# Softplus of a state-space kernel: its raw values copied to SBUF first, Exp and Ln kept in du, one clip for two row blocks

## The reference

```python
u = silu(conv(x @ W_in))
dbl = u @ W_x                      # 64 columns for dt, 16 for B, 16 for C
delta = softplus(dt @ W_dt + b_dt)
h = exp(delta * A) * h + (delta * u) * B      # over 2048 -> 4 x 512 tokens
y = sum over the 16 states of h * C
y = (y + u * Dp) * silu(res)
out = y @ W_out
```

## Time and profile before

| | |
|---|---|
| median of 3 runs | 2071.01 us (2067.32 to 2074.3) |
| profiled execution: its own time | 2073.18 us |
| its span, first to last instruction | 2071.5 us |
| mean granted TensorE clock | 0.971 of full speed |
| TensorE, matmuls | 1850.7 us busy, 89% |
| VectorE | 1564.5 us, 76% |
| ScalarE | 1464.7 us, 71% |
| GpSimd | 1538.3 us, 74% |

### The profile page before, as it was taken

How to read it: one execution, slowest core, us unless ns; L and a number is a source line. 1 busy time by engine, 2 the same in 40 slices (tenths; PEclk the granted TensorE clock), 3 DMA queues, 4 the chain that set the end, 5 groups by cost and what they waited for, 6 DMA issues and landing times.

```text
span 2071.5 us, 31985 instructions
## 1 busy us (share of the span) xinstructions
PE 1850.7 (89%) x12240; PEld 1465.2 (71%) x12240; DVE 1564.5 (76%) x1703; ACT 1464.7 (71%) x2467; POOL 1538.3 (74%) x896
## 2 busy tenths in 40 slices
PE   6989899999999999999999999999898986779994
PEld 3447677777777777777777777777677775669893
DVE  1358989798989897979798988888888887752232
ACT  0268888888888888888878787878797884613231
POOL 0039898889898988888888888888989896750331
PEclk9989999999999999999999999999999998899997
DMA  7211111111111111110111111111111112152542
GB/s 248 101 51 43 52 43 61 43 62 43 62 43 62 43 61 43 48 55 34 62 41 63 41 63 42 63 41 63 42 63 41 53 52 72 62 178 85 226 144 91
DMA packets 46394, 144.27 MB, mean 70 GB/s; under 512 B 7009, under 2 KB 18529, under 8 KB 42914
## 3 DMA queue, kind: packets, MB, share of 16 engines
q1 hardware_dynamic: 41538, 114.97, 16.2%
q0 software_dynamic: 4704, 27.27, 3.7%
HBM read 119.67 MB, written 22.54 MB: 69 GB/s over the span
## 4 chain that ended last, share of the span: by engine, by line
PE 52%; DVE 19%; issue 12%; ACT 12%; POOL 2%; DMA 2%; SPq 0%; DVEq 0%; POOLq 0%; ACTq 0%
PE b_ps L1316 12%; DVE hid L1043 10%; PE y_all L1327 9%; ACT dub_t L694 6%; ACT hid L681 5%; DVE u L851 4%; PE bank_b L1199 3%; PE bank_a L1449 3%; PE y_all L1118 3%; PE bank_b L1214 3%; PE bank_a L1223 3%; PE b_ps L1434 2%; PE y_all L1434 2%; PE bank_a L1247 2%; PE bank_a L1214 2%
## 5 line engine op out<-in xcount | busy, mean ns | idle before, releaser
L1043 DVE TENSOR_TENSOR_SCAN hid<-hid,b_ps 128x512 f32<-128x512 f32 x1024 | 1218.3, 1210 | 243.2 <-PE b_ps L1316 222.8
L504 POOL TENSOR_TENSOR hid<-hid,c_rep 128x1024 f32<-128x1024 f32 x512 | 1210.3, 2383 | 221.5 <-DVE hid L1043 221.5
L1316 PEld LDWEIGHTS b_ps<-ident,dub_t 128*128 128x128 f32 x4096 | 488.7, 143 | 375.5 <-issue 231.1
L1316 PE MATMUL b_ps<-ident,dub_t 128*128 128x128 f32 x4096 | 634.9, 278 | 78.9 <-DVE hid L1043 74.9
L681 ACT ACTIVATE hid<-delta,neg_a 128x512 f32<-128x512 f32 x1024 | 652.7, 710 | 0.2
L1327 PE MATMUL y_all<-ident,hid 128*128 128x128 f32 x4096 | 620.6, 275 | 3.8 <-POOL hid L504 3.8
L694 ACT ACTIVATE dub_t<-du_t,b_t 128x512 f32<-128x512 f32 x768 | 490.2, 711 | 54.8 <-PE b_ps L1316 53.1
L1327 PEld LDWEIGHTS y_all<-ident,hid 128*128 128x128 f32 x4096 | 485.7, 143 | 4.8 <-POOL hid L504 4.8
L495 POOL TENSOR_SCALAR dub_t<-du_t,b_t 128x512 f32<-128x512 f32 x256 | 173.8, 707 | 0.0
L1199 PE MATMUL bank_b<-xn,w_in_sb 128*128 128x512 f32 x256 | 134.5, 612 | 15.6 <-DVE xn L838 12.5
L851 DVE SCALAR_TENSOR_TENSOR u<-bank_b,conv_w_sb,u 128x511 f32<-128x511 f32 (+2 forms) x192 | 139.4, 726 | 0.7
(11 more groups left out here) (210 smaller groups left out, 1613.1 us busy)
## 6 DMA issues: line engine op xcount, KB each, us to landing
c_rep<-bc_dram SPq DMA_DIRECT2D x128, 512.0 KB, 3.6
hid<-x_t SPq DMA_DIRECT2D x4, 2048.0 KB, 8.8
xt<-x_dram SPq DMA_DIRECT2D x15, 512.0 KB, 3.6
x_dram<-x_out SPq DMA_DIRECT2D x15, 512.0 KB, 2.9
z_dram<-du SPq DMA_DIRECT2D x2, 1408.0 KB, 18.9
y_dram<-hid SPq DMA_DIRECT2D x22, 128.0 KB, 2.0
h_dram<-hid SPq DMA_DIRECT2D x4, 512.0 KB, 3.9
x_dram<-hid SPq DMA_DIRECT2D x3, 512.0 KB, 2.7
```

The source lines that it names most:

```text
L504: nc.gpsimd.tensor_tensor(part, part, c_rep[:, n % 2, s % GROUP, :].unsqueeze(1) .broadcast_to([P, HALF, SEQ]), ALU.mult).then_inc(hc_read ...
L1043: nc.vector.tensor_tensor_scan(hid[:, i % RING, d, :], hid[:, i % RING, d, :], b_ps[d % 2][:, :], 0.0, ALU.mult, ALU.add)\
L1316: last = nc.tensor.transpose(b_ps[d % 2][:, c * P:(c + 1) * P], dub_t[:, i % DUB, c, d * P:(d + 1) * P], ident[:, :])
```

## The change

ScalarE copies each W_dt product from PSUM to `delta` (its own semaphore `delta_in`), and that copy frees the bank for all that waited for the clip before. For each half (two row blocks) Exp then goes from `delta` to `du`, Ln in place in `du`, each as one instruction of 1024 elements a partition. The clip takes both operands from SBUF (`delta` and `du`), also one instruction for a half. ScalarE does all of this in one place of its list, ahead of the B products of state 9. The slots move: W_dt products 2 and 3 to (7, 0) and (7, 1), clips to (7, 1) and (7, 3), the norm's spread to (8, 1), normalise to (8, 2), `times_u` of the first half behind the first C product of state 7, and of the second half behind the first C product of state 8. The wait for `du` to be free goes from `times_u` to Exp.

```diff
@@ GpSimd
                         pool.wait_ge(delta_ready, NI * k + HALF * (half + 1))
                         if k:
                             pool.wait_ge(dut_done, TC * k)
-                        else:
-                            pool.wait_ge(z_zeroed, 2 * 16)
...
-                                if live(k + 1) and (s, half) == (6, 1):
+                                if live(k + 1) and (s, half) == (7, 0):
                                     times_u(k + 1, 0)
-                                if live(k + 1) and (s, half) == (7, 1):
+                                if live(k + 1) and (s, half) == (8, 0):
                                     times_u(k + 1, 1)
@@ ScalarE
-                    def delta_exp(k, d):
+                    def delta_copy(k, d):
                         act.wait_ge(wdt_done, NI * k + d + 1)
-                        nc.scalar.activation(delta[:, k % 2, d, :], (bank_a if d % 2 == 0 else bank_b)[:, :], ACT.Exp)\
-                            .then_inc(exp_ready, 1)
-
-                    def delta_log(k, d):
-                        act.wait_ge(exp_ready, NI * k + d + 1)
-                        nc.scalar.activation(delta[:, k % 2, d, :], delta[:, k % 2, d, :], ACT.Ln, bias=1.0).then_inc(log_ready, 1)
+                        nc.scalar.activation(delta[:, k % 2, d, :], (bank_a if d % 2 == 0 else bank_b)[:, :], ACT.Copy).then_inc(delta_in, 1)
+
+                    def delta_exp(k, half):
+                        rows = slice(half * HALF, (half + 1) * HALF)
+                        act.wait_ge(delta_in, NI * k + HALF * (half + 1))
+                        if k:
+                            act.wait_ge(dut_done, TC * k)
+                        else:
+                            act.wait_ge(z_zeroed, 2 * 16)
+                        nc.scalar.activation(du[:, rows, :], delta[:, k % 2, rows, :], ACT.Exp).then_inc(exp_ready, 1)
+
+                    def delta_log(k, half):
+                        rows = slice(half * HALF, (half + 1) * HALF)
+                        act.wait_ge(exp_ready, 2 * k + half + 1)
+                        nc.scalar.activation(du[:, rows, :], du[:, rows, :], ACT.Ln, bias=1.0).then_inc(log_ready, 1)
...
                             if s == 8 and live(k + 1):
-                                delta_exp(k + 1, 0)
-                                delta_exp(k + 1, 1)
-                                delta_log(k + 1, 0)
-                                delta_log(k + 1, 1)
+                                for half in range(2):
+                                    delta_copy(k + 1, 2 * half)
+                                    delta_copy(k + 1, 2 * half + 1)
+                                    delta_exp(k + 1, half)
+                                    delta_log(k + 1, half)
...
-                            if s == 8 and live(k + 1):
-                                delta_exp(k + 1, 2)
-                                delta_exp(k + 1, 3)
-                                delta_log(k + 1, 2)
-                                delta_log(k + 1, 3)
@@ VectorE
-                    def softplus(k, d):
-                        dve.wait_ge(log_ready, NI * k + d + 1)
-                        nc.vector.scalar_tensor_tensor(delta[:, k % 2, d, :], (bank_a if d % 2 == 0 else bank_b)[:, :], 60.0,
-                                                       delta[:, k % 2, d, :], ALU.max, ALU.min).then_inc(delta_ready, 1)
+                    def softplus(k, half):
+                        rows = slice(half * HALF, (half + 1) * HALF)
+                        dve.wait_ge(log_ready, 2 * k + half + 1)
+                        nc.vector.scalar_tensor_tensor(delta[:, k % 2, rows, :], delta[:, k % 2, rows, :], 60.0, du[:, rows, :],
+                                                       ALU.max, ALU.min).then_inc(delta_ready, HALF)
...
-                    SOFTPLUS_AT = {(7, 0): 0, (7, 1): 1, (8, 0): 2, (8, 1): 3}
+                    SOFTPLUS_AT = {(7, 1): 0, (7, 3): 1}
...
-                                if live(k + 2) and at == (8, 3):
+                                if live(k + 2) and at == (8, 2):
                                     normalize(k + 2)
@@ TensorE (delta_in for delta_ready also in du_turn, back and h_turn)
                         if k:
-                            pe.wait_ge(delta_ready, NI * k)
+                            pe.wait_ge(delta_in, NI * k)
...
                         if d >= 2:
-                            pe.wait_ge(delta_ready, NI * k + d - 1)
+                            pe.wait_ge(delta_in, NI * k + d - 1)
...
-                    WDT_AT = {(6, 1): 0, (6, 2): 1, (7, 1): 2, (7, 2): 3}
+                    WDT_AT = {(6, 1): 0, (6, 2): 1, (7, 0): 2, (7, 1): 3}
...
-                                if live(k + 2) and at == (8, 2):
+                                if live(k + 2) and at == (8, 1):
                                     spread_norm(k + 2)
```

More of the change, by code:

```diff
@@ L205, in build @@
             wdt_done = sem("wdt_done")
+            delta_in = sem("delta_in")
             exp_ready = sem("exp_ready")
@@ L1252, in du_turn @@
                             pe.wait_ge(du_ready, 2 * (k + 1))
-                            pe.wait_ge(delta_ready, NI * k + 3)
+                            pe.wait_ge(delta_in, NI * k + 3)
                             if k >= 2:
@@ L1265, in back @@
                         if dc == 0 and not live(k + 2):
-                            pe.wait_ge(delta_ready, NI * STEPS)
+                            pe.wait_ge(delta_in, NI * STEPS)
                             if k:
@@ L1273, in back @@
                         if dc == 2 and live(k + 2):
-                            pe.wait_ge(delta_ready, NI * (k + 2) + 3)
+                            pe.wait_ge(delta_in, NI * (k + 2) + 3)
                         if dc == 2 and not live(k + 2) and k:
```

## The result

The changed kernel took 2082.93 us (median of 4 runs, 2077.37 to 2085.82); the kernel before took 2069.16 us beside it (4 runs, 2064.63 to 2074.30). The ratio is 1.0065, 95% interval 1.0045 to 1.0084: slower by 0.65%. The number lies inside the range given (2048 to 2083), at its very end, but outside the likeliest case's own range (2062 to 2078), and the case forecast, no change that can be measured, did not happen.

The account below looks back on a forecast made before the run. No engine was full; each slot lasted as long as the slower of TensorE's and VectorE's lists. 9 x (1.64 - 1.6) + 5 x (1.76 - 1.6) = 1.2 us gained, about 0.8 in all, gave 2070 us, range 2048 to 2083.

Parts of the forecast that it names:

- the likeliest case: Whole kernel: a gain of about 0.8 us, about 2070 us, own range 2062 to 2078, chance 0.55.
- The bound and what is removed: TensorE's stalls for the clip at the third W_dt product, back 2 and the norm's spread go: 3.1 us a step.
- the walk: Part-by-part pass through one step, engine by engine; TensorE reaches the du turn at (9,2) about 2.7 us earlier if unobstructed.
- ScalarE: Four narrow copies and four wide instructions of 1.1 add 2.3 us a step, hidden ahead of the clips.
- GpSimd's chain: GpSimd from state 6's last product to du complete: 14.40 us + x; a step gains 1.64 - x, or 1.76 - x.
- x: Time the two wide clips take from GpSimd a step: 1.4 to 1.8 us, taken as 1.6, bounds 0 and 2.2.
- rival 2: GpSimd from state 7 to du's second half becomes the bound; x 2.2 to 2.4, 2078 to 2081 us; chance 0.18.
- VectorE waits about 2 us, but this is hidden: At the second clip, if GpSimd issues first; TensorE is then at the turn at 724.4, still before du.
- The last step: Last of the sixteen steps, without normalise, GpSimd behind all the way: loses up to 0.4 us.
- The clock: Granted clock dips in five of fourteen steps; the change shifts this, from no dips (-8) to all fourteen (+14 us).
- rival 3: TensorE's idle stretches at (8,2) or (9,2) grow to 3 us, more steps dip: up to 2085 us; chance 0.10.

## Why the prediction was wrong

**The bound and what is removed: right.** The three bank stalls are gone. Once du is in time and no clip is held up, a step is 102.0 to 102.4 long instead of 104.4, and 101.7 with clips of one operand, which is the 2.7 us that the walk gave.

**ScalarE: right.** Each wide Exp and Ln lasts 1.06 (taken 1.1), and no clip of the full steps waits for one.

**GpSimd's chain: right in form.** The prediction had 14.40 us + x, with gains of 1.64 - x and 1.76 - x; at x = 0 the runs gave 1.62 and 1.71. In the steps with the dip x is 0.90 + 1.04 = 1.94, so a loss of 0.18 was due, and 106.23 against 106.07 is 0.16.

**The size of x: this is the step that failed**, and with it the sign. The prediction took 1.6 as the likeliest, since "a short instruction slips in between two of GpSimd's in about 0.4 us that cost nothing", from the earlier trace rows. That row was an instruction of 0.40 us that reads one tensor, and it was carried over to clips of 1.2 that read two. Nor does it show a free place in between: the two of these instructions that met the products at 1796.95 lasted 1.57 and 2.42, and each ended 0.15 us after the product beside it. The clips cost GpSimd 0.9 to 1.04 each wherever they got in, with no discount: in the step of the result section without a dip 1.16 (du waiting for the clip) + 0.99 = 2.15. The chain is 16.3 to 16.6 us long, which the prediction's own mark of 16.2 calls rival 2. The rival had the right place and mechanism, with a chance of 0.18; its x of 2.2 to 2.4 was a little too large. With the measured x the prediction's own formulas give, over the 13 steps, 7 x (2.15 - 1.64) + 6 x (1.94 - 1.76) = 4.7 us lost instead of 1.2 gained. That settles the sign, but it is only about half of the 9.2 measured; the other half is the clock, below.

**"VectorE waits about 2 us, but this is hidden": wrong as well.** The prediction allowed this for the second clip only; it happened to the first, in 8 of 14 steps, and du's first half had to wait for it. Nor is it hidden: TensorE has scans to feed behind it and pauses 3.2 us, and this cost 2.9 us a step even where du was in time. For the second clip, where it alone had two SBUF operands, the same: 4.31 us of pause. The prediction put this wait of TensorE at nothing; it is most of the 23.4 us more ahead of the B transposes.

**The last step: mis-sized.** "Loses up to 0.4" was 3.9. The new order alone accounts for 2.1 of it (102.58 against 100.45), with du behind its turn.

**The clock: in part rival 3.** One more dip after the squares, 1.8 us. Beyond that, what the rival had named: pauses of over 3 us in one piece, behind which the clock falls. Windows of 2 us from two turns at which TensorE had waited 3.17 (us, TensorE's busy us, clock, DMA share, GB/s):

```profile
624.30:626.30 2.00, 2.00 (x18) 1.00 0.00 0
626.30:628.30 2.00, 2.00 (x20) 1.00 0.00 0
307.21:309.21 2.00, 2.00 (x15) 0.79 0.00 0
309.21:311.21 2.00, 2.00 (x11) 0.50 0.00 0
```

Behind the turn at 624.30 the clock stayed, behind that at 307.21 it fell to half. It fell behind four of the six waits of 3.15 to 3.32, and the steps that follow these four are 105.8 long, where the others of their kind are 104.95 to 105.2; that is about 3 us. What decides between the two wasn't found, and it isn't the length of the wait alone: with only the first clip on two operands it fell behind a wait of 2.36 (turn at 1456.84; 0.50 from 1458.84 to 1460.84), and in the changed kernel's repeat it stayed at 1.00 behind waits of 3.40 and 3.44 (turns at 1470.78 and 204.52). Nor is it settled why the version with du's old places has no dip at all; the last 8 of its 32.6 us can't be counted on.

**The Trainium skill**, "SBUF — State Buffer", section "Who interferes with whom", says that an instruction of VectorE with two SBUF inputs contends with one of GpSimd that reads SBUF, that the second to issue is blocked fully, and that a `tensor_reduce` never contends. The runs agree: 1.19 us for each reduce, and 38.6 us between the two clips. In one point they differ: it says that the order of issue decides, and the clip issued at 924.39 let the product that started at 924.64 go first. The prediction cited the rule and then granted a discount from a row of another instruction. The rule speaks of two instructions; what a queue of them does to the one that waits, 3.73 to 8.27 us for 1.2 us of work, is what the experiments add.

## What to carry over

An operand moved from PSUM to SBUF can cost more than the stall it removes: look up what GpSimd reads beside the instruction, charge the full overlap in both directions, and as the worst case charge the waiting engine with every GpSimd instruction queued behind the current one. If such an instruction can't be avoided, put GpSimd's consumer of its result directly behind the current product in GpSimd's list, so that GpSimd itself waits and leaves the gap; and make it one wide instruction rather than two narrow ones. An engine's reserve ahead of a hand-over (here 4.8 us) can be spent once: moving du later cost 0.26% alone, two SBUF operands with du's old places gained 1.6%, and both together lost 0.65%.

## What the runs showed of the hardware that I had not expected

- VectorE, waiting with two SBUF operands for GpSimd to finish an instruction, is not sure of the next gap. It lost one C product (3.73 us for 1.2 us of work), a rest of du and one more (5.05), or the whole queue until GpSimd ran dry (7.73, 8.27). In other places it won the first gap with much the same wait: 0.3 us of waiting lost at 924.39 of the changed kernel, and 0.3 us won at 930.29; with the second clip alone, 1.5 us won (2.60 in all) and 1.7 lost (5.05). Which gap is given to whom stays open.
- Two such instructions back to back on VectorE are split by one of GpSimd: 3.60 us for a pair that takes 1.27 where it isn't split.
- TensorE's clock fell to half (0.50 in the windows above) behind pauses of 3.2 us in some places and not in others, behind one of 2.36 and not behind one of 3.44, while behind waits of 1.4 us, in nearly every step of the kernel without a second operand, the matmuls kept their 0.60.
